# Two-layer graph transformer on one core: the second part of the turn in another order, PSUM banks dealt anew, the vo copies on the vector engine

## What is computed

```
# layer 0, for each graph
nx = ln1(x);  q, k, v = nx@wq+bq, nx@wk+bk, nx@wv+bv          # 8 heads of 32
attn = softmax(q@k.T/sqrt(32) + bias)                          # -inf where adj == 0
x1 = x + (attn@v)@wo + bo
x2 = x1 + gelu(ln2(x1)@w1 + b1)@w2 + b2                        # hidden 1024
# layer 1, for each graph
w = softmax(where(adj == 0, -inf, (x2@Wq)@(x2@Wk).T/16))
y = x2 + (w@(x2@Wv))@Wo + bo1
out = ln3(y)
```

## Time and profile before

| | |
|---|---|
| median of 3 executions | 939.46 us |
| profiled execution, its own time | 938.92 us |
| its span, first to last instruction | 936.4 us |
| TensorE busy | 910.6 us, 97% |
| VectorE, ScalarE, GpSimd busy | 689.6, 629.1, 385.0 us |
| mean granted TensorE clock | 0.992 of full speed |

### The profile page before, as it was taken

One profiled execution on the slowest core, in us unless ns is written; L12 is line 12 of the kernel. 1 busy time (PEld: TensorE's weight loads), 2 busy tenths in 40 slices (PEclk: granted clock), 3 DMA queues, 4 the chain that ended last, 5 costly groups with the idle time before them and its releaser, 6 DMA issues.

```text
span 936.4 us, 22265 instructions
## 1 busy us (share of the span) xinstructions
PE 910.6 (97%) x7495; PEld 812.9 (87%) x7495; DVE 689.6 (74%) x2575; ACT 629.1 (67%) x1855; POOL 385.0 (41%) x257
## 2 busy tenths in 40 slices
PE   9889999999999999999999999999999999998995
PEld 8777898988889898888989889898988989898894
DVE  6686867869587786958779595877958687785735
ACT  5585958668485766848677585867758586674751
POOL 3425153543616354261535426253451626344221
PEclk9999999999999999999999999999999999999998
DMA  8101000100101001010100101010010100000000
GB/s 260 34 2 35 2 23 24 35 24 5 51 0 34 22 22 34 0 56 0 34 22 22 34 0 35 21 34 22 22 34 0 34 22 28 11 24 1 24 1 34
DMA packets 29727, 26.27 MB, mean 28 GB/s; under 512 B 1127, under 2 KB 29437, under 8 KB 29693
## 3 DMA queue, kind: packets, MB, share of 16 engines
q1 hardware_dynamic: 29676, 25.83, 8.7%
q10 hardware_dynamic: 16, 0.00, 0.0%
HBM read 17.44 MB, written 8.39 MB: 28 GB/s over the span
## 4 chain that ended last, share of the span: by engine, by line
PE 89%; DVE 4%; ACT 3%; issue 2%; POOL 2%; DVEq 0%; POOLq 0%
PE bank L325 21%; PE bank L327 19%; PE bank L326 19%; PE bank L488 5%; PE bank L469 5%; PE bank L461 4%; PE bank L480 3%; PE bank L560 3%; PE bank L588 3%; PE bank L541 2%; PE bank L500 1%; PE bank L411 1%; ACT bank L798 1%; PE bank L377 1%; PE bank L578 1%
## 5 line engine op out<-in xcount | busy, mean ns | idle before, releaser
L798 ACT ACTIVATE bank<-p_s,neg_max 128x128 f32<-128x128 f32 x512 | 182.3, 356 | 23.5 <-DVE neg_max L1085 23.3
L1415 POOL TENSOR_TENSOR rstd<-ve,minus_half 128x4 f32<-128x4 f32 (+1 forms) x51 | 51.1, 1003 | 307.7 <-DVE ve L1049 307.7
L325 PE MATMUL bank<-w_hi,hT_hi 128*128 128x256 f32 x512 | 147.1, 287 | 0.0
L327 PE MATMUL bank<-w_hi,hT_lo 128*128 128x256 f32 x512 | 144.2, 282 | 0.0
L326 PE MATMUL bank<-w_lo,hT_hi 128*128 128x256 f32 x512 | 144.1, 282 | 0.0
L1085 DVE CUSTOM_DVE_ANT_0 p_s<-bank,bias 128x128 f32<-128x128 f32 x512 | 112.6, 286 | 7.7 <-PE bank L461 7.6
L325 PE MATMUL bank<-n2T_hi,w_hi 128*128 128x512 f32 (+1 forms) x272 | 113.1, 416 | 3.4 <-DVE qk_lo L983 3.3
L814 ACT ACTIVATE bank<-bank,vec_cols 128x512 f32<-128x512 f32 (+1 forms) x136 | 86.4, 635 | 39.0 <-PE bank L327 36.0
L327 PE MATMUL bank<-n2T_hi,w_lo 128*128 128x512 f32 (+1 forms) x272 | 103.8, 382 | 0.0
L326 PE MATMUL bank<-n2T_lo,w_hi 128*128 128x512 f32 (+1 forms) x272 | 103.5, 380 | 0.0
L325 PEld LDWEIGHTS bank<-w_hi,hT_hi 128*128 128x128 f32 x512 | 96.4, 188 | 1.8
(11 more groups left out here) (204 smaller groups left out, 2372.6 us busy)
## 6 DMA issues: line engine op xcount, KB each, us to landing
xs<-in_x SPq DMA_DIRECT2D x15, 512.0 KB, 3.7
out<-y SPq DMA_DIRECT2D x15, 512.0 KB, 2.9
adj_i<-in_adj SPq DMA_DIRECT2D x15, 256.0 KB, 2.8
x2T_f<-in_L_gnn_w SPq DMA_DIRECT2D x1, 512.0 KB, 7.2
tT<-in_L_gnn_w SPq DMA_DIRECT2D x1, 512.0 KB, 8.8
y<-in_L_gnn_w SPq DMA_DIRECT2D x1, 512.0 KB, 6.7
vo<-in_L_gnn_w SPq DMA_DIRECT2D x1, 512.0 KB, 8.9
x_bo<-in_x SPq DMA_DIRECT2D x1, 256.0 KB, 2.9
```

Source lines behind the costliest of these rows:

```text
L325: mm(out, a_hi, b_hi, start=first, stop=False)
L327: return mm(out, a_lo, b_hi, start=False, stop=last)
L798: last = run(bank[r][:, NODES * place:NODES * place + NODES], p_s[:, r, place, :], ACT.Exp, scale=-1.0, bias=neg_max[:, r, place:place + 1 ...
L1415: P.tensor_tensor(t["rstd"][:, 0:k], t["ve"][:, 0:k], minus_half[:, 0:k], ALU.pow).then_inc(ln_pool[n], 1)
```

## The change

In the second part of the turn TensorE's order becomes `project_q`, `scores1`, `scores`, `project_v(gp, 1)`, `vo_project`, `p1_transpose`, `n2_transpose`, `attend1`. The banks of the steps that share 4 to 7 are dealt anew: `mlp_up` takes (6, 7, 4, 5), `mlp_down` (6, 7), norm 1's transposes and `attend1` (4, 5). The waits follow: `n2_transpose` now waits for both vo copies (`dve_vo`), since it writes the banks that they read; the first products of `mlp_up` wait for one half of n2T each. The scalar engine no longer copies vo; the vector engine copies both pairs. On both engines the steps stand in another order. Amounts of work are the same otherwise. In the prologue two weight transposes and one weight product change banks, and the wait for `qk1` stands ahead of `mlp_up(0, 2)` in place of `mlp_up(0, 3)`.

```diff
@@ -176,16 +176,16 @@
 
         bank = [ctx.enter_context(nc.psum_tensor(f"bank{i}", [128, 512], f32)) for i in range(8)]
         av_bank, wo_bank = 0, 1
-        up_bank = (4, 5, 6, 7)
-        down_bank = (4, 5)
-        nx_bank, k_bank, q_bank, v_bank = (6, 7), (5, 6), (5, 4), (6, 5)
+        up_bank = (6, 7, 4, 5)
+        down_bank = (6, 7)
+        nx_bank, k_bank, q_bank, v_bank = (4, 5), (5, 6), (5, 4), (6, 5)
         x2_bank, t_bank, s1_bank, vo_bank = (7, 4), (7, 4), 5, (6, 7)
-        p1_bank, av1_bank, n2_bank = 4, (6, 7), (6, 7)
+        p1_bank, av1_bank, n2_bank = 4, (4, 5), (6, 7)
         usual_banks = dict(up=up_bank, down=down_bank, n2=n2_bank, x2=x2_bank, t=t_bank, s1=s1_bank, vo=vo_bank,
                            p1=p1_bank, av1=av1_bank)
         own_banks = dict(up=(0, 1, 2, 3), down=(0,), n2=(2, 3), x2=(2, 3), t=(2, 3), s1=1, vo=(0,), p1=3, av1=(2,))
 
-        l1_bank, l1_mm_bank = (5, 4, 5), (7, 5)
+        l1_bank, l1_mm_bank = (6, 7, 7), (4, 7)
 
...
@@ -379,7 +379,7 @@
 
             def l1_transpose(i):
                 pe.wait_ge(w_load["l1"], L1_ALL)
-                pe.wait_ge(*((dve_shift, 6), (dve_shift, 7), (dve_l1, 1))[i])
+                pe.wait_ge(*((act_v, 1), (dve_shift, 8), (act_l1, 1))[i])
                 for c in range(KT):
                     for r in range(KT):
...
@@ -390,6 +390,7 @@
                 if k == 0:
                     pe.wait_ge(dve_l1, 1)
                     pe.wait_ge(act_l1, 1)
+                    pe.wait_ge(act_q, 4)
                 else:
                     pe.wait_ge(act_l1, 2)
...
@@ -403,8 +404,7 @@
 
             def norm_transpose(g):
                 if isinstance(g, int) and g == 1:
-                    pe.wait_ge(act_v, 1)
-                    pe.wait_ge(dve_shift, 8)
+                    pe.wait_ge(dve_shift, 7)
                 pe.wait_ge(ln_dve[1], ln_end(g))
                 for t in range(KT):
...
@@ -439,6 +437,8 @@
             def project_v(g, q):
                 if q == 0:
                     pe.wait_ge(dve_nxT, 2 * g + 2)
+                    if not (isinstance(g, int) and g < 2):
+                        pe.wait_ge(dve_x2, pair0(g - 2) + 1)
                 for b in (2 * q, 2 * q + 1):
                     for t in range(KT):
...
@@ -489,11 +489,9 @@
                                   start=(t == 0), stop=(t == KT - 1))
                 last.then_inc(pe_wo, 1)
 
-            def n2_transpose(g, P, B):
-                if P:
-                    pe.wait_ge(act_k, 2 * g + 4)
-                if B:
-                    pe.wait_ge(act_t, g)
+            def n2_transpose(g, B):
+                if B:
+                    pe.wait_ge(dve_vo, pair0(g))
                 pe.wait_ge(ln_dve[2], ln_end(g))
                 for t in range(KT):
...
@@ -501,23 +499,17 @@
                     last.then_inc(pe_n2T, 1)
 
 
-            def mlp_up(g, j, A):
-                if j == 0:
-                    pe.wait_ge(dve_n2T, 2 * g + 2)
-                if is_last(g):
-                    if j >= 4:
-                        pe.wait_ge(dve_h, HT * g + j - 3)
-                elif j == 0:
-                    pe.wait_ge(act_p1T, g)
-                elif j == 1 and A:
-                    pe.wait_ge(act_v, pair0(g + 1) + size(g + 1) // 2)
-                elif j == 2:
-                    pe.wait_ge(dve_y, graph0(g) - 2 if not isinstance(g, int) or g > 1 else graph0(g))
-                elif j == 3:
-                    pe.wait_ge(dve_y, graph0(g))
-                elif j >= 4:
+            def mlp_up(g, j):
+                if not is_last(g):
+                    if j == 2:
+                        pe.wait_ge(dve_y, graph0(g) - 2 if not isinstance(g, int) or g > 1 else graph0(g))
+                    elif j == 3:
+                        pe.wait_ge(dve_y, graph0(g))
+                if j >= 4:
                     pe.wait_ge(dve_h, HT * g + j - 3)
                 for t in range(KT):
+                    if j == 0:
+                        pe.wait_ge(dve_n2T, 2 * g + t + 1)
                     last = mm3(bank[at("up", g)[j % 4]][:, toks(g)], both(w1_p, ALL, t, nodes(j)), both(n2T, ALL, t, toks(g)),
                                t == 0, t == KT - 1)
...
@@ -536,6 +528,8 @@
 
             def x2_transpose(g):
                 pe.wait_ge(dve_x2, pair0(g) + size(g) // 2)
+                if isinstance(g, int) and g == 0:
+                    pe.wait_ge(dve_lo, SPLIT["vo1"])
                 for t in range(KT):
                     for b in range(size(g)):
...
@@ -561,11 +555,9 @@
                                   start=(t == 0), stop=(t == KT - 1))
                 last.then_inc(pe_s1, 1)
 
-            def vo_project(g, q, A):
+            def vo_project(g, q):
                 if isinstance(g, int) and g == 0:
                     pe.wait_ge(dve_lo, SPLIT["vo1"])
-                if A:
-                    pe.wait_ge(dve_n2T, 2 * g + 3 + q)
                 for b in (2 * q, 2 * q + 1):
                     for t in range(KT):
...
@@ -578,12 +570,18 @@
                     last = tr(bank[at("p1", g)][:, nodes(b)], home("p1", g)[:, b, :], ident[:, :])
                 last.then_inc(pe_p1T, 1)
 
-            def attend1(g):
+            def attend1(g, P=False):
                 pe.wait_ge(act_p1T, g + 1)
-                pe.wait_ge(act_vo, g + 1)
-                if size(g) > 2:
-                    pe.wait_ge(dve_vo, g)
+                if is_last(g):
+                    pe.wait_ge(act_vo, 2)
+                elif isinstance(g, int) and g == GROUPS - 2:
+                    pe.wait_ge(dve_vo, pair0(g) + 1)
+                    pe.wait_ge(act_vo, 1)
+                else:
+                    pe.wait_ge(dve_vo, pair0(g + 1))
                 for q in pairs(g):
+                    if q == 1 and P:
+                        pe.wait_ge(act_v, pair0(g + 2) + 2)
                     for b in (2 * q, 2 * q + 1):
                         last = mm(bank[at("av1", g)[q]][:, row(b)], home("p1T", g)[:, b, :], home("vo", g)[:, b, :], start=True, stop=True)
...
@@ -595,23 +593,24 @@
                 first = isinstance(gb, int) and gb == 0
                 if first:
                     pe.wait_ge(dve_lo, SPLIT["w1"])
+                    pe.wait_ge(act_v, pair0(1) + 2)
                 for j in range(4):
-                    if first and j == 3:
+                    if first and j == 2:
                         pe.wait_ge(dve_lo, SPLIT["qk1"])
-                    mlp_up(gb, j, A)
+                    mlp_up(gb, j)
                 if A:
                     p_transpose(ga, 0)
                 if B:
-                    mlp_up(gb, 4, A)
+                    mlp_up(gb, 4)
...
@@ -640,53 +639,53 @@
                 if P:
                     project_q(gp, 0)
                     project_q(gp, 1, B)
-                if A:
-                    n2_transpose(ga, P, B)
                 if B:
                     scores1(gb, P)
                 if P:
                     scores(gp, 0)
-                if B:
-                    for q in pairs(gb):
-                        vo_project(gb, q, A)
-                    p1_transpose(gb)
                 if P and size(gp) > 2:
                     if B:
                         pe.wait_ge(dve_s1, gb + 1)
                     project_v(gp, 1)
                 if B:
-                    attend1(gb)
+                    for q in pairs(gb):
+                        vo_project(gb, q)
+                    p1_transpose(gb)
+                if A:
+                    n2_transpose(ga, B)
+                if B:
+                    attend1(gb, P and size(gp) > 2)
 
             def last_turn(ga, gb):
 
                 for j in range(4):
-                    mlp_up(gb, j, True)
+                    mlp_up(gb, j)
                 p_transpose(ga, 0)
-                mlp_up(gb, 4, True)
+                mlp_up(gb, 4)
                 attend(ga, 0)
-                mlp_up(gb, 5, True)
...
@@ -884,19 +883,18 @@
                 if P:
                     q_copy(gp, 0)
                     q_copy(gp, 1)
+                if B:
+                    exps1(gb)
+                if P:
+                    if size(gp) > 2:
+                        v_copy(gp, 1)
+                    exps(gp, 0, 0)
+                    exps(gp, 0, 1)
+                if B:
+                    p1T_copy(gb)
                 if A:
                     n2T_copy(ga)
-                if B:
-                    exps1(gb)
-                if P:
-                    exps(gp, 0, 0)
-                if B:
-                    vo_copy(gb)
-                    p1T_copy(gb)
-                if P:
-                    exps(gp, 0, 1)
-                    if size(gp) > 2:
-                        v_copy(gp, 1)
+                if P:
                     exps(gp, 0, 2)
                     exps(gp, 0, 3)
...
@@ -1271,22 +1269,24 @@
                     norm2(ga)
                 if B:
                     t_copy(gb)
-                if A:
-                    n2T_low(ga)
```

(43 more changed lines are left out.)

16 lines of the change are left out of this document (7 added, 9 removed).

## The result

| | before | after |
|---|---|---|
| median of 4 executions, us | 938.59 (936.04 to 943.14) | 950.66 (950.05 to 951.71) |
| span of the profiled execution, us | 936.4 | 948.3 |
| a turn of the loop, us | 55.17 | 55.97 |

The ratio of the medians is 1.0132 (95%: 1.011 to 1.0155): the changed kernel is 1.3% slower, 12.1 us. The prediction was 952 in a range of 946 to 957.

What follows compares the result with a forecast made beforehand. TensorE, busy 97% of the span, was taken to bound the kernel. Thirteen turns at 0.76 give 9.9; less 0.35, plus 0.6, 0.7 and 1.6, +12.4 on 938.92: 951.4, with the median's 0.54 952 us, range 946 to 957.

Steps and rivals of the forecast that it cites:

- What bounds: Loop turns: TensorE is busy for 55.16 of 55.16 us, so each unfinished wait lengthens the turn by its whole length.
- The wait of the v products: After layer 0's scores: v waits 0.18 us for biased1's last maximum, since it writes the bank that biased1 reads.
- The products: v and vo are 36 matmuls of one form: v takes 1.48 us, vo's 24 cost 2.96.
- The wait of norm 2's transposes: After p1's transposes: 0.60 us until the second vo copy has freed banks 6 and 7; the largest term.
- S: The start of layer 0's scores, from which the prediction counts the times of the turn's end.
- What comes behind: From norm 2's transposes to the next turn: p1T and n2T's first half each in time by 0.3 us, y priced at nothing.
- The ends: Turns outside the loop: (3,2,1) 0.76 us less 0.35; (16,15,14) +0.6; first turn +0.7 at mlp_up(0, 2) and +1.6 at its end.
- Not slower: Rival, 4%: both waits are over in time and fewer changes of form save under 0.1 us each; 936 to 940 us.
- only one wait shows: Rival, 13%: transition costs hide the v wait and the first turn's terms; 15 turns at 0.58 less 0.35, 947 us.
- The chain behind the transposes: Rival, 12%: VectorE or ScalarE over 0.3 us late, so the next turn's first product waits for dve_n2T; 955 to 957 us.
- the clock after the stop: TensorE's clock falls after the first turn's long stop: two to six microseconds at half speed cost 1 to 3.
- The clock swings: Rival, 1%: the stretch from layer 0's scores to the turn's end runs at half speed in 15 turns; +112, 1064 us.

Runs made afterwards that it cites:

- the halved release: Changed kernel, norm 2's transposes waiting in two steps: first four for the first vo copy alone, other four for the second; 947.87 us, ratio 1.0094 to the kernel before.
- the second profile of before: The kernel before, run once more unchanged for its profile; 937.49 us.
- the stop of 4.0 us: The kernel before with the wait for qk1 ahead of mlp_up(0, 2) in place of mlp_up(0, 3); 939.87 us, ratio 1.0016.
- the two kernels whose stop is gone: The kernel before with qk1 made earlier, 936.73 us; the changed kernel with that, v behind p1's transposes and vo copies ahead of the fourth biased, 935.12 us.

## Why the prediction was right, step by step

- **What bounds.** Right. TensorE had no gap in the loop before, so every wait went into the turn at full length: a turn is 0.80 longer (predicted 0.76), the loop 9.57 (12 x 0.76 = 9.1).
- **The wait of the v products.** 0.18 predicted, 0.18 to 0.19 measured (1.10 to 1.29). It would be "a wait on record 14 times", I wrote; the record shows none, since the pipeline's modelled end covers it. Only the difference of starts tells it.
- **The products.** 4.44 predicted, 4.37 measured.
- **The wait of norm 2's transposes.** 0.60 predicted; p1's step grew from 0.35 to 1.04, so 0.69. VectorE began the second copy at S+5.88, against 5.92 predicted: products and fourth biased do meet there. The 0.09 is three small misses: the products were through 0.06 earlier, which lengthens the wait, the copy ended 0.04 earlier (S+6.57), which shortens it, and its end took 0.13 to reach TensorE and not the 0.06 read from another pair of rows. The transposes so start at S+6.70 instead of 6.67, and take 0.92 behind their wait instead of 0.87. The next turn begins at S+9.16, against 9.08; the turn as a whole is 0.04 over the prediction.
- **What comes behind.** p1T and n2T were in time, as predicted, and `attend1` and the first `mlp_up` have no wait. p1T's copy ended at S+7.17 (predicted 7.20), 0.45 before `attend1` and not 0.34; with the halved release it became the wait.
- **The ends.** Turn (3,2,1): +0.29 measured, 0.41 predicted. Turn (16,15,14): +0.38 against +0.6, inside its bounds. Its end is as predicted: 7.11 us from the scores to the next turn before, 8.61 with the change, less the 0.87 is +0.63. But its wait for tT is 1.05 long and not 1.27, a step that the sum left out. First turn: from the scores to the next turn 8.02 (predicted 8.05), with the predicted wait for p1T (0.72). The predicted wait for n2T_lo is in no list: `attend1`'s step takes 1.20 (96.79 to 97.99) and not 0.78 as before, so again only the starts tell it. With `mlp_up(0, 2)` behind the stop +2.3 in all, which the second profile of before confirms with 2.35. In the first pair of profiles only +1.64 shows: the stop's end came 2.19 us earlier (51.53 against 53.72), and the low clock behind it took 1.48 (44.11 less 42.63); both differ from run to run without the change.
- **The rivals.** "Not slower" and "only one wait shows" fell with the two waits at 0.18 and 0.69. "The chain behind the transposes" did not decide in the loop. Its other half, the clock after the stop, happened, but as well without the change. "The clock swings" fell: behind 55.8 us the granted clock is 1.00 to the end, with two waits in each turn. The rule of the Trainium skill, "TensorE: Matmul & The Clock Gate", section "A second HAM failure mode: psum-queue depth-cycling", has no case here: a wait of 0.2 and one of 0.7 in 56 us did not start a swing.

The sum was 12.4; measured are 11.9 between the spans and 12.1 between the medians. That it is this close is partly luck: the loop came out 0.5 over its term and the ends 0.3 under theirs, and in the first pair of profiles the first turn shows 0.7 too little by chance of the clock. Against the second profile of before (935.7) the spans differ by 12.6. The executions of the kernel before alone lie between 936.04 and 943.14, and the interval of the ratio is 10.3 to 14.5 us.

## What to carry to other kernels

When a step moves on a full engine, ask two things: what it will wait for in the new place, and what its latency covered in the old one; v moved alone cost more (1.10 per turn) than the whole change (0.80), because it had covered the copy of p1T. Lay the short transposes and the copies so that a long product covers each copy out of PSUM until TensorE needs it: here 1.50 us of v products cover 1.0 (from the end of the vo products to the freed bank) and, with the 0.35 of p1's transposes, 1.3 (from their start to p1T). Read a wait from differences of starts: one of 0.18 us stood in no list of waits.

## What the runs showed of the hardware

- The end of a wait reached TensorE after 0.05 to 0.07 us for neg_max to v, qk_lo to `mlp_up` and p1T to `attend1`, in the loop too. From the vo copy to norm 2's transposes it was 0.05 to 0.06 in the changed kernel's three turns outside the hardware loop, but 0.12 to 0.14 in the twelve turns of the loop, and the same with the copy later still. Where the second half of the transposes waited by itself (the halved release), it was 0.05, in the loop. With the two waits exchanged it was 0.14 to 0.15 everywhere, and with the first copy on ScalarE 0.24 to 0.25 in the loop and 0.10 in the two turns outside it that wait there. Why is open.
- `attend1` takes 1.62 to 1.65 us when it starts from a wait for p1T, 1.54 when it doesn't; the transposes 0.90 to 0.93 against 0.87 to 0.88. In these kernels a wait in front of a group costs 0.03 to 0.1 beyond itself.
- TensorE's clock behind the stop of 3.3 us: 1.00 within it and for 0.8 to 1.4 us of work after it, then 0.50 for 3.4 us, in both profiles of the changed kernel and in one of two of before (with the stop of 4.0 us it fell within the stop, at about 53.7, and stayed there for 6.8 us); not at all in the one profile of each of the two kernels whose stop is gone. The Trainium skill, "TensorE: Matmul & The Clock Gate", section "What's actually happening", says that the gate is set by how busy the engine has been recently; a fall that comes late in the stop or after it fits that. Why one profile escaped, no run here tells.
- The low clock early in the prologue (0.50 between 20 and 28 us) lasted 3.4 us in one profile of each of the two kernels and 6.8 in the other. With the longer one the stop's end came 2.2 us later in the kernel before (53.72 against 51.48) and 2.0 later in the changed one (53.55 against 51.53).
